# Moving the second background count of a unit into the unit's products, in a graph-network kernel on one Trainium2 core

## The reference, cut to what matters

```python
seg = edge_type * n + dst
agg = segment_sum(x[src], seg, 34 * n)
cnt = segment_sum(ones, seg, 34 * n)
mean = agg.reshape(34, n, -1) / maximum(cnt, 1.0).reshape(34, n, 1)
h1 = einsum('rni,rio->no', mean, W_rel) + x @ W_root + b_rgcn
```

## Time and profile before

| | |
|---|---|
| median of 3 runs | 1991.13 us (1988.38 to 1992.34) |
| the profiled execution | 1990.38 us |
| its span, from the first to the last instruction | 1988.7 us |
| TensorE busy | 1710.9 us, 86% of the span |
| the 15 key units, from the first's sums to the sums behind the last | 593.84 to 990.55 us |
| granted TensorE clock, mean over the span | 0.926 of full speed |

### The profile page before, as it was taken

How to read it: one execution, slowest core, us unless ns; L and a number is a source line. 1 busy time by engine, 2 the same in 40 slices (tenths; PEclk the granted TensorE clock), 3 DMA queues, 4 the chain that set the end, 5 groups by cost and what they waited for, 6 DMA issues and landing times. The chain is left out here.

```text
span 1988.7 us, 31024 instructions
## 1 busy us (share of the span) xinstructions
PE 1710.9 (86%) x10102; PEld 1570.3 (79%) x10103; DVE 1150.2 (58%) x1890; ACT 629.2 (32%) x839; POOL 352.4 (18%) x301
## 2 busy tenths in 40 slices
PE   2765279999989888888873998999998999899988
PEld 1643269899878777777763898899998999899988
DVE  7979777777766545555563646355343455444463
ACT  3000135565554444444443221222112222222220
POOL 5020136456452322222230000000000000000000
PEclk9876589999999989989995999899998999999999
DMA  4000249798885666666564111222012221231111
GB/s 151 24 17 0 85 156 271 209 270 261 213 260 160 157 166 183 191 174 185 162 165 120 47 49 53 81 81 72 22 55 72 72 71 32 58 84 55 50 47 47
DMA packets 84489, 230.08 MB, mean 116 GB/s; under 512 B 10350, under 2 KB 22641, under 8 KB 84434
## 3 DMA queue, kind: packets, MB, share of 16 engines
q1 hardware_dynamic: 65090, 158.14, 25.0%
q0 software_dynamic: 19344, 71.18, 15.5%
HBM read 190.01 MB, written 39.28 MB: 115 GB/s over the span
## 5 line engine op out<-in xcount | busy, mean ns | idle before, releaser
L923 PE MATMUL layers_ps_o<-layers_w_hi,layers_g_hi 128*125 128x384 f32 (+1 forms) x1040 | 362.4, 348 | 4.5 <-DVE layers_w_lo L787 3.2
L924 PE MATMUL layers_ps_o<-layers_w_lo,layers_g_hi 128*125 128x384 f32 (+1 forms) x1040 | 360.7, 347 | 0.0
L925 PE MATMUL layers_ps_o<-layers_w_hi,layers_g_lo 128*125 128x384 f32 (+1 forms) x1040 | 360.3, 346 | 0.0
L948 PE MATMUL layers_ps_g<-a,h_hi 125*128 125x316 f32 x840 | 196.7, 316 | 55.2 <-DVE h_lo L409 42.3
L1856 PE MATMUL l_means_ps<-l_means_w_hi,l_means_g_hi 128*128 128x512 f32 (+1 forms) x912 | 235.4, 339 | 0.5
L1856 PE MATMUL l_means_ps<-l_means_w_hi,l_means_g_lo 128*128 128x512 f32 (+1 forms) x912 | 235.3, 339 | 0.0
L1856 PE MATMUL l_means_ps<-l_means_w_lo,l_means_g_hi 128*128 128x512 f32 (+1 forms) x912 | 234.3, 338 | 0.0
L1567 ACT CAST l_means_w_hi<-l_means_w_raw 128x768 fp32r<-128x768 f32 x209 | 174.3, 837 | 188.9 <-PE l_means_ps L1856 182.5
L1840 PE MATMUL l_means_ps<-l_means_pick,l_means_e_hi 128*128 128x256 f32 (+1 forms) x612 | 187.5, 331 | 47.7 <-issue 30.3
L1728 DVE TENSOR_TENSOR l_means_w_lo<-l_means_w_raw,l_means_w_hi 128x768 fp32r<-128x768 f32 x209 | 190.4, 953 | 37.1 <-ACT l_means_w_hi L1567 34.3
L923 PEld LDWEIGHTS layers_ps_o<-layers_w_hi,layers_g_hi 128*125 128x125 f32 x1040 | 194.0, 187 | 14.9 <-issue 5.0
(11 more groups left out here) (318 smaller groups left out, 2481.7 us busy)
## 6 DMA issues: line engine op xcount, KB each, us to landing
l_means_w_raw<-in_L_gnn_W_rel SPq DMA_DIRECT2D x210, 384.0 KB
layers_w_raw<-in_L_gnn_w_rel SPq DMA_DIRECT2D x39, 384.0 KB, 3.5
layers_w_raw<-in_L_gnn_w_rel SPq DMA_DIRECT2D x21, 448.0 KB, 3.9
layers_a_raw<-adj SPq DMA_DIRECT2D x9, 769.0 KB
layers_w_raw<-in_L_gnn_W SPq DMA_DIRECT2D x18, 384.0 KB, 5.1
l_means_list_now<-targets SPq DMA_DIRECT2D x35, 192.0 KB
layers_w_raw<-in_L_gnn_w_root SPq DMA_DIRECT2D x13, 384.0 KB, 3.9
layers_w_raw<-in_L_gnn_w_root SPq DMA_DIRECT2D x7, 448.0 KB, 3.9
```

Of the source, the lines that this page charges most:

```text
L923: t.matmul(out, g_hi[:, f, rows], w_hi[:, f, cols], start=(f == 0), stop=False)
L924: t.matmul(out, g_hi[:, f, rows], w_lo[:, f, cols], start=False, stop=False)
L925: mm = t.matmul(out, g_lo[:, f, rows], w_hi[:, f, cols], start=False, stop=(f == fc - 1))
L948: mm = t.matmul(ps_g[:, buf, at:at + PART[p]], rows[:, k, f * 128:(f + 1) * 128], a[:, k, cols], start=(k == 0 and part == 0), stop=(k == ...
```

## The change

Both keys of a unit are counted inside its products: the first ahead of the fifth chunk, the second ahead of the sixth. ScalarE copies both ahead of `take_y`. Nothing else is changed: the same matmuls, copies and casts are issued, in another order.

```diff
@@ ScalarE, one_unit
                 if key_pair is not None:
-                    copy_key(key_number(2 * key_pair))
+                    for b in range(2):
+                        copy_key(key_number(2 * key_pair + b))
...
                 if_third(act, third, take_y)
-                if key_pair is not None:
-                    copy_key(key_number(2 * key_pair + 1))
@@ TensorE, one_unit
                     for f in range(fc):
-                        if f == fc - 1 and key_pair is not None:
-                            count_key(key_number(2 * key_pair))
+                        if f >= fc - 2 and key_pair is not None:
+                            count_key(key_number(2 * key_pair + f - (fc - 2)))
@@ TensorE, the loop over the key units
                 one_unit(unit(n + list_units), n)
-                count_key(key_number(2 * n + 1))
```

## The result

The changed kernel took 2022.62 us (median of 4 runs, 2021.74 to 2023.91) against 1989.76 us: a ratio of 1.0165, 95% interval 1.0148 to 1.0183. It is 33 us slower. The forecast was 2028 us.

A forecast was written before the change was run, and what follows sets the result against it. TensorE and its instruction stream were taken to set the time in the key units. +29.1 us from the new order and +8 from the clock, +37 on 1991.13, gave 2028 us, 1.9% slower; range 2004 to 2052.

The forecast's parts named there:

- The place and the order: Key units: first count 1.10 us ahead of the fifth chunk; then cast, copy, table read, second count, sixth chunk, next sums.
- The pause: TensorE between fifth and sixth chunk: 1.65 us to the copy's end plus 4.59 of reading and counting, 6.24 us.
- The next unit's start: Gap ahead of the next unit's sums, 1.54 us before, hidden under the sixth chunk's products and priced at zero.
- the rival that this start isn't hidden: Stream reaches the loop's end only when the sixth chunk is nearly over: +23 us, 2051 us; 8%.
- The clock: TensorE at half clock behind the longer pauses in the key units: +8 us, bounds -27 and +27.
- The sum: Key units: +29.1 us from 11 two-tile units at +1.72 and 4 three-tile at +2.55, plus 8 for half clock: +37.
- One sign named in advance: Trace of a two-tile unit: time from its sums to the next, 25.4 us, up to 27.1 and what half clock adds.
- the stream is stopped by the wait for the copy, and can't run ahead through the second count: Kernel before, second count: table read only after ScalarE's copy, so it takes 4.52 us against the first count's 1.10.
- That the second count would be hidden like the first: Rival, second count in its new place: 46 us gained, 1945 us, down to 1918 with no half-clock stretch; 6%.
- neither without it: Rival, key units: the half-clock stretch falls into the pause, +29 - 27 = +2, 1993 us; 8%.
- nor with twice the cost: Rival, key units: the half-clock stretch lasts twice as long, +29 + 27 = +56, 2047 us; 14%.

The follow-up runs named there:

- The early copy: The changed kernel, with ScalarE copying the first key behind its fourth cast and ahead of the fifth: 1959.94 us, 0.9857 of the kernel before.
- the early read: The changed kernel, with count_key reading its two table entries ahead of the wait for the copy: 1987.34 us, 0.9994 of the kernel before.
- The kept-busy array: The changed kernel with 16 unneeded matmuls in each pause ahead of the second count: 1994.35 us, 1.003 of the kernel before.
- the run with the read ahead of the wait: The kernel before, with only the table entries read ahead of the wait for the copy: 1982.48 us, 0.9965 of the kernel before.
- the run with both edits: The changed kernel, first key copied ahead of the fifth cast and table read ahead of the wait: 1936.87 us, 0.9738 of the kernel before.
- the run with two chunks between the counts: The changed kernel, table read ahead of the wait, first key counted ahead of the fourth chunk, copies earlier: 1930.71 us, 0.9708 of the kernel before.
- the run with three chunks between: The changed kernel, table read ahead of the wait, first key counted ahead of the third chunk, copies earlier: 1933.89 us, 0.973 of the kernel before.

## Why the prediction was right

**The place and the order.** Each step that it named is in the trace of after: the first count hidden ahead of the fifth chunk, the cast and the copy ahead of the second count, the table read behind the copy, the sixth chunk late, the next sums without a gap. The early copy shows by experiment that the order on ScalarE, cast before copy, is one cause of the pause, and the early read that the reading is another.

**The pause: mis-sized, 5.6 instead of 6.24 us.** From the fifth chunk's end to the copy's end the forecast had 1.65 us; it was 761.25 - 759.85 = 1.40. From there to the sixth chunk it had 4.59; it was 765.46 - 761.25 = 4.21, with tiles 0.8 us apart where the kernel before, under the same code, had 0.84 and 1.00:

```profile
751.69 0.32 PE L1815 MATMUL l_means_ps<-l_means_is_dst,l_means_is_src 128*125 x1 [0.26 <-issue]
752.53 0.32 PE L1815 MATMUL l_means_ps<-l_means_is_dst,l_means_is_src 128*125 x1 [0.52 <-issue]
753.53 0.32 PE L1815 MATMUL l_means_ps<-l_means_is_dst,l_means_is_src 128*125 x1 [0.68 <-issue]
```

Over all units the pause is 5.65 us with two tiles and 5.58 us with three (start of the sixth chunk less start of the fifth, less a chunk's 2.12 or 3.2 us). Why the same instructions came faster here was not tested.

**The next unit's start: right.** 1.54 us were priced at zero, and 769.03 follows 768.68 at the pitch of the products. So the rival that this start isn't hidden is out.

**The clock: the term was 8 us; it comes out at about 6.** The sums take 98.4 us before (from 593.84 on, so without the six early matmuls) and 78.2 us after, the chunks behind the last count after 63.4 us. At full clock the sums are 4.31 us in two-tile and 6.31 us in three-tile units, together 72.7 (72.0 without the six), and the chunks 11 x 2.16 + 4 x 3.22 = 36.6 us. So half clock costs 98.4 - 72.0 = 26.4 us before, and 5.5 + 26.8 = 32.3 us after: 5.9 us more. The kept-busy array gave 26 of those 32 back. The 8 was a value chosen between bounds of -27 and +27 us, not derived, so that it came this near is partly luck. The prediction didn't say either where the stretch would lie: most of it moved from the sums to the sixth chunk.

**The sum.** In the key units +30.5 us: 0.7 from the six matmuls, 5.9 from the clock and 24 from the order, where the forecast had 8 and 29.1. The pauses make 11 x 0.6 + 4 x 0.3 = 8 us less than forecast. In the other direction go the first counts, 21.6 us in all against 20.4 (two of them, of 1.67 and 2.42 us, stand behind a table read of 0.8 instead of 0.3 us), and the second counts of the kernel before, 62.1 us in all where the two units shown gave 11 x 4.52 + 4 x 3.31 = 63. One sign named in advance did not come in the unit shown: from its sums to the next ones took 769.03 - 743.20 = 25.8 us, not 27.1 and more. The unit of 25.4 us that it was to be compared with had run 2.75 us longer in its sums than at full clock (7.06 us for 36 matmuls), the new one loses 2.0 us to half clock, and its pause is 0.6 us shorter than forecast.

**What was wrong in the reasoning.** The step "the stream is stopped by the wait for the copy, and can't run ahead through the second count" overstated the wait. It holds after the change: the stream got to the wait at 757.8 and stood there until 761.3. In the kernel before it stood about half a microsecond (749.2 to 749.7, the second of the two times in its row), and the run with the read ahead of the wait gained 5 us, where the same reading had promised 23. The second count was dear because the stream works about 4.2 us on a count and had spent most of its lead on the first: it read the table 2.9 us ahead of the first count, and 1.4 us ahead of the second (749.8 to 751.27). The forecast didn't suffer: it used the measured lengths and needed the wait only where the changed kernel has it.

The stream's arrivals at the wait, after and before:

```profile
L1808 PEldq ALU_OP  x1: 32/32/32, 757.8 to 757.8; - x1
```
```profile
L1809 PEldq FUSED_REGOPS  x2: 37/42/48, 744.9 to 749.2; - x2
```

**The rivals.** That the second count would be hidden like the first was ruled out by the order on ScalarE, as argued. The runs that hide it have an early copy, two or three chunks between the counts and the table read ahead of the wait, and with all three the gain is 57 us; whether it takes the third was not tested. The pause kept its half-clock stretch, neither without it nor with twice the cost.

## What to carry to other kernels

A short piece of work with a run-time loop is cheap on TensorE only if its instruction stream is far enough ahead: here the stream works 4.2 us on 0.9 us of matmuls, and it was some 3 us ahead where a count was hidden. Two such pieces must stand so far apart that the stream can get ahead again; here one chunk of 2.2 us was too little and two, 4.3 us, were enough. Before moving work past a wait, look at what the instruction that releases it waits for on its own engine: here a copy of 0.42 us stood behind a cast that waited for exactly the matmuls that were to cover it.

## What the runs showed of the hardware that was not expected

The order of two neighbouring ScalarE instructions was worth 61 us, 3%. Of the 61.9 us by which the key units shrank, the pause explains about 43 and the clock about 19. Half clock behind a pause of 5.6 us could mostly be avoided with unneeded matmuls in the pause, at a net gain of 26 us.

With pauses of 2.1 to 2.6 us, in the run with both edits, the granted clock was 1.00 in most of the key units; with pauses of about 3.3 us, in the run with the early copy alone, it was 0.96. No border can be read from that: in the run with two chunks between the counts, a first count of 2.56 us, with gaps between its tiles of 0.5 us at most, was followed by such a stretch too:

```profile
826.00:830.50 4.50, 3.99 (x14) 0.66 0.81 238
```

The stream's lead at the table read of a hidden count was 2.8 to 3.1 us, whether the previous count lay in the unit before, three chunks back or two, except once, 3.8 us, behind that stretch at half clock. One table read took 0.30 us as a rule and up to 1.17 us in the run with three chunks between.
